# Row sums taken out of the values products, a normalisation in turned 32x32 blocks, score products dealt out over the PSUM banks, ScalarE's root and an earlier part of the ranks, in a six-stage decoder on one core

## What is computed

```python
x = _layernorm(x + _L0_attn_ref(x, ...))    # stage a: 16 heads of 128, window 64
x = _layernorm(x + _L0_xattn_ref(x, ctx))   # stage b: 16 heads of 16, causal
x = _layernorm(x + _L0_ffn_ref(x, ...))     # stage c: 8 experts, top 2
x = _layernorm(x + _L1_attn_ref(x, ...))    # stage d: 32 heads of 8, 8 kv heads, causal
x = _layernorm(x + _L1_xattn_ref(x, ctx))   # stage e: latent attention, 1601 keys
x = _layernorm(x + _L1_ffn_ref(x, ...))     # stage f: 16 heads of 16 with rms norms, then stage g: 8 experts
```

```python
scores = einsum('bhqd,bhkd->bhqk', qh, kh) * hd ** -0.5
attn   = softmax(where(causal, scores, min))
out    = einsum('bhqk,bhkd->bhqd', attn, vh)
```

## Time and profile before

| | before |
|---|---|
| median of 3 runs | 1814.74 us |
| lowest and highest | 1813.94, 1819.88 us |
| the profiled execution's own time | 1813.53 us |
| span of its trace | 1812.3 us |
| mean granted TensorE clock | 0.976 |
| PE busy | 1701.6 us (94%) |
| PEld busy | 1497.3 us (83%) |
| DVE busy | 1442.3 us (80%) |
| ACT busy | 1198.2 us (66%) |
| POOL busy | 810.8 us (45%) |

### The profile page before, as it was taken

One profiled execution on the slowest core, in us unless ns is written; L12 is line 12 of the kernel. 1 busy time (PEld: TensorE's weight loads), 2 busy tenths in 40 slices (PEclk: granted clock), 3 DMA queues, 4 the chain that ended last, 5 costly groups with the idle time before them and its releaser, 6 DMA issues.

```text
span 1812.3 us, 42783 instructions
## 1 busy us (share of the span) xinstructions
PE 1701.6 (94%) x15680; PEld 1497.3 (83%) x15680; DVE 1442.3 (80%) x3572; ACT 1198.2 (66%) x2998; POOL 810.8 (45%) x720
## 2 busy tenths in 40 slices
PE   7999999989999999899999999999999997897994
PEld 6999977758867776799999999999999996774883
DVE  5777757859856866799999999999999997686995
ACT  5766754326634543588888888888888885532663
POOL 5744422248844432444444444444444431224874
PEclk8999999989999999899999999999999999998998
DMA  5000019232338000000000000000000003302233
GB/s 175 25 1 1 1 72 361 79 99 45 54 73 265 11 3 2 24 12 13 13 12 13 30 13 13 13 13 13 12 13 1 1 2 134 158 2 86 45 54 70
DMA packets 51867, 91.74 MB, mean 51 GB/s; under 512 B 4592, under 2 KB 43632, under 8 KB 49232
## 3 DMA queue, kind: packets, MB, share of 16 engines
q1 hardware_dynamic: 42928, 78.16, 12.9%
q0 software_dynamic: 8160, 10.29, 3.7%
q10 hardware_dynamic: 576, 0.56, 0.1%
HBM read 56.13 MB, written 32.87 MB: 49 GB/s over the span
## 4 chain that ended last, share of the span: by engine, by line
PE 76%; DVE 11%; issue 4%; ACT 4%; DMA 3%; POOL 2%; SPq 0%; DVEq 0%; ACTq 0%; POOLq 0%
PE bank L100 63%; PE bank L2647 10%; DVE a_t L707 1%; PE bank L1923 1%; PE bank L1175 1%; DVE a_t L704 1%; DMA g_sums<-g_y,g_xs 1%; DMA c_sums<-c_y,c_xs 1%; POOL c_rows L1789 1%; PE bank L1895 1%; PE bank L505 1%; DVE tiny L133 1%; ACT a_OT_hi L614 0%; ACT a_P L631 0%; DVE b_nm L1444 0%
## 5 line engine op out<-in xcount | busy, mean ns | idle before, releaser
L2747 ACT ACTIVATE e_P<-bank,e_st 128x496 f32<-128x496 f32 (+2 forms) x512 | 306.3, 600 | 32.5 <-DVE e_st L2829 32.5
L2825 DVE TENSOR_REDUCE e_st<-bank 128x1 f32<-128x496 f32 (+2 forms) x512 | 288.3, 571 | 35.0 <-PE bank L100 24.8
L2848 DVE TENSOR_TENSOR e_PT_lo<-bank,e_PT_hi 128x512 fp32r<-128x512 f32 (+1 forms) x448 | 281.0, 644 | 30.9 <-ACT e_PT_hi L2767 29.9
L2647 PE MATMUL bank<-ident,e_P 128*128 128x128 f32 (+1 forms) x1664 | 257.1, 274 | 4.0 <-DVE e_PT_lo L2848 3.9
L2767 ACT CAST e_PT_hi<-bank 128x512 fp32r<-128x512 f32 (+1 forms) x448 | 247.4, 554 | 18.3 <-PE bank L2647 10.8
L100 PE MATMUL bank<-e_PT_hi,e_kv 128*128 128x256 f32 (+1 forms) x832 | 232.1, 300 | 3.1 <-DVE e_cx_lo L2855 3.1
L100 PE MATMUL bank<-e_PT_lo,e_kv 128*128 128x256 f32 (+1 forms) x832 | 214.9, 279 | 0.0
L100 PE MATMUL bank<-e_KT,e_qk_hi 128*128 128x496 f32 (+2 forms) x512 | 208.5, 407 | 6.5 <-ACT e_P L2747 3.4
L2647 PEld LDWEIGHTS bank<-ident,e_P 128*128 128x128 f32 (+1 forms) x1664 | 197.7, 140 | 17.5 <-issue 3.1
L100 PE MATMUL bank<-e_KT,e_qk_lo 128*128 128x496 f32 (+2 forms) x512 | 178.5, 349 | 0.0
L100 PEld LDWEIGHTS bank<-e_PT_hi,e_kv 128*128 128x128 f32 (+1 forms) x832 | 156.9, 189 | 8.5 <-DVE e_cx_lo L2855 3.8
(11 more groups left out here) (489 smaller groups left out, 5353.7 us busy)
## 6 DMA issues: line engine op xcount, KB each, us to landing
c_wall<-in_c_w SPq DMA_DIRECT2D x8, 1536.0 KB, 19.0
g_wall<-in_g_w SPq DMA_DIRECT2D x8, 1536.0 KB, 19.3
c_rows<-normed SPq DMA_DIRECT2D x9, 1040.0 KB, 12.9
g_rows<-normed SPq DMA_DIRECT2D x9, 1040.0 KB, 13.4
e_stage<-in_e_w SPq DMA_DIRECT2D x16, 416.0 KB, 3.2
c_xs<-c_rows SPq DMA_DIRECT2D x23, 130.0 KB
g_xs<-g_rows SPq DMA_DIRECT2D x23, 130.0 KB
landing<-in_a_wo SPq DMA_DIRECT2D x2, 1024.0 KB, 6.1
```

What stands on the lines that cost most here:

```text
L2647: last = pe.transpose(o[0:rows, c * SEQ + i * P:c * SEQ + (i + 1) * P], p[:, i, k0:k0 + rows], ident[:])
L2747: act.activation(Pm[u % 2][:, i, STARTS[j]:STARTS[j] + n], bank[score_bank[j]][:, 0:n], ACT.Exp, bias=s[:, i, 4:5], accum_out=s[:, i, j:j ...
L2825: last = dve.tensor_reduce(s[:, i, j:j + 1], bank[score_bank[j]][:, 0:PIECES[j]], AX.X, ALU.max)
L2848: dve.tensor_tensor(lo, bank[tb_bank[at % 2]][0:rows, 0:n * SEQ].rearrange("p (c n) -> p c n", c=n), hi.bitcast(F32), ALU.subtract).then_i ...
```

## The change

1. `values`: the eight products with `ones` go, and so do that tile and its memsets. Two columns per V slot are set to one (two strided memsets of GpSimd), so that in a block of 32 rows the 16 rows that hold no output hold the row sums. The units of a pair or four are shared between two accumulations, `outs[0]` and `outs[1]`, the two halves of bank 6. The first unit's values wait for `inverted`, which the first instruction of `normalise` now signals.
2. `normalise`: VectorE turns the whole bank in blocks of 32 x 32 (`transpose`, PSUM to `lifted`, 128 x 512), takes two small reciprocals of the sums (8 elements of each partition in b and f, 16 in d), multiplies in two instructions of 128 elements, and turns the result back into O (128 x 256), with two waits on its own semaphore between. The halves do the same on half of the columns each.
3. `scores`: where both kinds of scores are made (58 of the 64 units), the 24 products go in six groups of four; a group has four different row tiles and four different banks, and each from the third on waits for the last product of the group two before it, so four waits in place of one.
4. `ranks(g)`: the products of ones for the tiles before n0 go ahead of the wait for `marked(g + 1)`; behind it stand two products.
5. `experts`: in c's norm of batch 0 and in `last_norms` ScalarE takes the root (`Sqrt`, with a dummy call ahead of it), VectorE the reciprocal and one `newton` step, in place of the guess and three steps.

```diff
         V = [A(f"V{i}", [P, 2, kv_heads, slot]) for i in range(2)]
-        ones = A("ones", [P, slot])
...
             PT = [A(f"PT{i}", [P, 3, 4, P])[:] for i in range(2)]
-        inv = [A(f"inv{i}", [P, SEQ]) for i in range(2)]
+        lifted = A("lifted", [P, 2 * SEQ])[:].rearrange("p (r q f) -> p r q f", r=2, f=32)
+        inv = A("inv", [P, 2, SEQ // 32, 16 // hd])
...
         A_BANK, B_BANK, OUT_BANK, SIDE = 0, 3, 6, 7
-        outs, sums = bank[OUT_BANK][:, 0:SEQ], bank[OUT_BANK][:, SEQ:2 * SEQ]
+        outs = [bank[OUT_BANK][:, r * SEQ:(r + 1) * SEQ] for r in range(2)]
...
-            def score(n, block, j, keys_first):
+            def score(n, block, j, keys_first, opens=False):
...
                 o = bank[(B_BANK if keys_first else A_BANK) + at][:, col * P:(col + 1) * P]
-                return mm(o, k if keys_first else q, q if keys_first else k, keys_first and j == 3, True)
+                return mm(o, k if keys_first else q, q if keys_first else k, opens, True)
+            def scores_of_both(n0, n1):
+                def queries(block, j):
+                    return score(n0, block, j, False)
+                def keys(block, j, opens=False):
+                    return score(n1, block, j, True, opens)
+                queries(0, 0)
+                queries(0, 1)
+                queries(0, 2)
+                keys(1, 3, True).then_inc(half_scored.sem, 1)
+                first = half_scored.step()
+                queries(1, 0)
+                queries(1, 1)
+                keys(0, 2, True)
+                keys(0, 3, True).then_inc(half_scored.sem, 1)
+                second = half_scored.step()
+                pe.wait_ge(half_scored.sem, first)
+                queries(2, 0)
+                keys(0, 1)
+                keys(1, 2)
+                queries(2, 3).then_inc(half_scored.sem, 1)
+                third = half_scored.step()
+                pe.wait_ge(half_scored.sem, second)
+                keys(0, 0)
+                keys(1, 1)
+                keys(2, 2)
+                queries(1, 3).then_inc(half_scored.sem, 1)
+                fourth = half_scored.step()
+                pe.wait_ge(half_scored.sem, third)
+                keys(1, 0)
+                keys(2, 1)
+                queries(1, 2)
+                queries(0, 3)
+                pe.wait_ge(half_scored.sem, fourth)
+                queries(2, 1)
+                queries(2, 2).then_inc(*scored0.up())
+                keys(2, 0)
+                keys(2, 3).then_inc(*scored1.up())
...
                         pe.wait_ge(*exped.at(2 * n1))
+                if n0 is not None and n1 is not None:
+                    scores_of_both(n0, n1)
+                    return
...
                     if n1 is not None:
-                        last = score(n1, block, 3, True)
+                        last = score(n1, block, 3, True, True)
...
                 p, v = PT[n % 2], V[b % 2]
-                first, final = x == 0, x == PER - 1
+                r, rest = divmod(x, PER // 2)
...
                     pe.wait_ge(*ones_made.at(1))
-                if first and n >= PER:
-                    pe.wait_ge(*o_made.at(n // PER))
-                for into in (outs, sums):
-                    for kt in range(2):
-                        for j in range(4):
-                            h = (4 * u + j) // rep
-                            w = v[:, kt, h, at:at + 32] if into is outs else ones[:, at:at + 32]
-                            o = into[32 * j:32 * j + 32, kt * P:2 * P]
-                            x = (p[:, 2, 3, :] if kt else p[:, 0:2, 3, :]) if j == 3 else (
-                                p[:, j, 2, :] if kt else p[:, j, 0:2, :])
-                            last = mm(o, w, x, first and into is outs and kt == 0, final)
+                if x == 0 and n >= PER:
+                    pe.wait_ge(*inverted.at(n // PER))
+                for kt in range(2):
+                    for j in range(4):
+                        w = v[:, kt, (4 * u + j) // rep, at:at + 32]
+                        o = outs[r][32 * j:32 * j + 32, kt * P:2 * P]
+                        seen = (p[:, 2, 3, :] if kt else p[:, 0:2, 3, :]) if j == 3 else (
+                            p[:, j, 2, :] if kt else p[:, j, 0:2, :])
+                        last = mm(o, w, seen, x == 0 and kt == 0, rest == PER // 2 - 1)
...
                     dve.wait_ge(*summed.at(b - 1))
+                rows = bank[OUT_BANK].rearrange("p (r q f) -> p r q f", r=2, f=32)
                 for n, cols in enumerate(halves(m)):
-                    dve.reciprocal(inv[m % 2][:, cols], sums[:, cols]).then_inc(*inverted.up())
+                    q = slice(cols.start // 32, cols.stop // 32)
+                    dve.transpose(lifted[:, :, q, :], rows[:, :, q, :]).then_inc(*inverted.up())
                     dve.wait_ge(*inverted.at(m + 1 + n))
-                    dve.tensor_tensor(O[b % 2][:, c, cols], outs[:, cols], inv[m % 2][:, cols],
-                                      ALU.mult).then_inc(*o_made.up())
+                    for r in range(2):
+                        last = dve.reciprocal(inv[:, r, q, :], lifted[:, r, q, 16 - 16 * r:32 - 16 * r:hd])
+                    last.then_inc(link.sem, 1)
+                    dve.wait_ge(link.sem, link.step())
+                    for r in range(2):
+                        x = slice(16 * r, 16 * r + 16)
+                        last = dve.tensor_tensor(lifted[:, 0, q, x].rearrange("p q (x d) -> p q x d", d=hd),
+                                                 lifted[:, r, q, x].rearrange("p q (x d) -> p q x d", d=hd),
+                                                 inv[:, r, q, :].unsqueeze(3).broadcast_to(
+                                                     [P, q.stop - q.start, 16 // hd, hd]), ALU.mult)
+                    last.then_inc(link.sem, 1)
+                    dve.wait_ge(link.sem, link.step())
+                    dve.transpose(O[b % 2][:, c, cols].rearrange("p (q f) -> p q f", f=32),
+                                  lifted[:, 0, q, :]).then_inc(*o_made.up())
...
                 pool.memset(NM[x][:], 0.0).then_inc(*cleared.up())
-            pool.memset(ones[:], 0.0).then_inc(*cleared.up())
-            pool.wait_ge(*cleared.at(2 + PER + 1))
-            pool.memset(ones[:, gap:gap + hd], 1.0).then_inc(*ones_made.up())
+            pool.wait_ge(*cleared.at(2 + PER))
+            for i in range(2):
+                last = pool.memset(V[i][:, :, :, gap - 16:gap + 17:32], 1.0)
+            last.then_inc(*ones_made.up())
...
             pe.wait_ge(*self.tables_made.at(1))
+        else:
+            pe.wait_ge(*self.marked.at(g))
+        for n in range(n0):
+            mm(o[:, n0 * E:n1 * E].rearrange("p (n e) -> p n e", e=E), self.ones[:],
+               self.either[:, n:n + 1, :].broadcast_to([P, n1 - n0, E]), n == 0, False)
         pe.wait_ge(*self.marked.at(g + 1))
-        last = mm(o[:, n0 * E:n1 * E], self.earlier[:], self.either[:, n0:n1, :], True, False)
-        for n in range(n1 - 1):
-            m = max(n0, n + 1)
-            last = mm(o[:, m * E:n1 * E].rearrange("p (n e) -> p n e", e=E), self.ones[:],
-                      self.either[:, n:n + 1, :].broadcast_to([P, n1 - m, E]), False, True)
-        last.then_inc(*self.ranked.up())
+        mm(o[:, n0 * E:n1 * E], self.earlier[:], self.either[:, n0:n1, :], n0 == 0, False)
+        mm(o[:, (n1 - 1) * E:n1 * E], self.ones[:], self.either[:, n0, :], False, True).then_inc(*self.ranked.up())
...
         last_scales, odd_normed, even_normed = S_("last_scales"), S_("odd_normed"), S_("even_normed")
+        spread_known, rooted = S_("q_projected"), S_("k_projected")
...
                     upper_w(i + 1, at, 1)
+            act.activation(silu[0][:, 0:1], ident[:, 0:1], ACT.Sqrt)
+            act.wait_ge(*spread_known.at(1))
             if following:
+                act.activation(tiny[0][:, 20:22], tiny[0][:, 16:18], ACT.Sqrt).then_inc(*rooted.up())
...
             else:
+                act.activation(normal[:, TILES:2 * TILES], normal[:, 0:TILES], ACT.Sqrt).then_inc(*rooted.up())
...
+            def norm_first(T):
+                mean = T[:, 12:16].rearrange("p (t s) -> p t s", s=2)
+                v, y, s = T[:, 16:18], T[:, 18:20], T[:, 20:22]
+                row_stats(0, T)
+                dve.wait_ge(link.sem, link.value)
+                dve.tensor_scalar(v, mean[:, :, 1], EPS, None, ALU.add).then_inc(*spread_known.up())
+                dve.wait_ge(*rooted.at(1))
+                then(dve.reciprocal(y, s))
+                newton(v, y, s)
+                dve.wait_ge(link.sem, link.value)
+                for i in range(2):
+                    normed_ = dve.tensor_scalar(X[:, i, :], X[:, i, :], T[:, 12 + 2 * i:13 + 2 * i], T[:, 18 + i:19 + i],
+                                                ALU.subtract, ALU.mult)
+                normed_.then_inc(x_normed, 1)
...
                 v, s = normal[:, 0:TILES], normal[:, TILES:2 * TILES]
```

(11 more changed lines are left out.)

## The result

| | before | after |
|---|---|---|
| median | 1814.74 us (5 runs, 1810.47 to 1819.88) | 1803.90 us (5 runs, 1799.83 to 1805.17) |
| ratio of the runs | | 0.9937, interval 0.9915 to 0.9959 |
| profiled execution: span, clock | 1812.3 us, 0.976 | 1802.7 us, 0.971 |

A forecast was written before the change was run, and what follows sets the result against it. TensorE was taken as the bound, with VectorE second. Terms 20.0 + 1.3 + 3.3 + 2.0 - 0.9 - 6.3 + 0.3 + 2.3 = 22.0 us off 1814.7 gave a forecast of 1793, range 1779 to 1805.

The forecast's parts named there:

- Rival C: Normalise is dearer and VectorE binds more widely: 24 calls at 0.9 us, half exposed, 10 less gain, 1803; chance 0.16.
- D (1804): Scores: the four waits expose more than the one did, 0.23 us dearer in 50 units, 11 less, 1804; chance 0.12.
- Ones products: TensorE-bound units of b, d and f: dropping the ones group gains its whole 0.67 us in each of 27.
- Score order: Scores: two exposed waits of 0.15 us replace one of 0.37, gaining 0.07 a unit (bounds 0.37 gained, 0.23 lost).
- floor: The 19 units of b, d and f whose mask products wait for VectorE's maxima: 4.64 us, forecast 4.57.
- Normalise: VectorE's normalise: 2.20 us before, priced at 2.04 in b and f and 2.14 in d, taken as 2.1.
- VectorE's limit: Where normalise and layernorm operations lie between maxima in b, d and f, VectorE becomes the bound: 6.3 us less gain.
- The pair of the earlier trace: Two neighbouring units from 620.78 to 631.85: 11.07 us before, forecast 10.6 as VectorE binds, gaining 0.5 instead of 1.5.
- Units with a turned layernorm: The 11 units where TensorE waits otherwise for VectorE or ScalarE, mostly for that layernorm's low part: 0.3 us each, 3.3 together.
- rival E: The granted clock falls in 23 thinned units, costing 30 us, 8 more than the gain: 1823, slower; chance 0.06.
- Ranks: Stages c and g: six of eight products move ahead of VectorE's mark, 0.2 us in each, 0.3 taken for both.
- Root: From v to X's scaling at c's end, 2.38 us becomes 1.25, 1.1 less; in g 1.2 less; together 2.3.

The follow-up runs named there:

- e6: The changed kernel with the turn of the maxima moved behind the iteration's single projection or output product; 1811.10 us, ratio 0.9988 to the kernel before.
- e1: The kernel before with part 3 alone, the new order of the score products; 1812.52 us, ratio 1.0001.
- e8: The changed kernel measured again, unaltered, on another chip; 1799.73 us, ratio 0.9940 to the kernel before.
- e4: The changed kernel with normalise turning the bank in place, so that its products read PSUM; 1795.02 us, ratio 0.9905 to the kernel before.
- e5: The changed kernel with 12 or 13 idle products in the last three iterations of b, d and f; 1797.37 us, ratio 0.9917 to the kernel before.
- e12: The kernel before with parts 1 and 2 alone, sums out of the values products and normalise in turned blocks; 1803.41 us, ratio 0.9968.
- e3: The kernel before with parts 4 and 5 alone, the earlier ranks products and the root on ScalarE; 1809.40 us, ratio 0.9984.
- e9: The changed kernel with both the in-place turn in PSUM and the idle products at the stages' ends; 1794.41 us, ratio 0.9907 to the kernel before.

## Why the prediction was right in sign and twice too large

The profiles differ by 9.6 us where 22.0 were forecast. By the milestones, with the prediction's terms shared out among the stages, the missing 12.4 are: 5.0 in d's units (8.5 forecast, 3.5 measured), 4.2 between d's last maxima and f (0.4 less forecast, 3.8 more measured), 4.0 behind f (1.7 less forecast, 2.3 more measured); b, f and the stretch from b to d gave 0.8 more than forecast.

The measured 1803.9 lies where the rivals C (1803) and D (1804) stood, and what they say did not happen: normalise costs what was priced, and the waits of the new order expose 0.27 in a unit where the old one lost 0.37. So it is luck that the range, drawn to reach past D, held the time.

- *Ones products: a wait that they covered.* I priced the group at 0.67 and let a unit gain all of it, "since everything up to the mask follows in TensorE's order". The price was right: in e6, with no turn behind them, the next product starts 0.78 behind the values, against 1.43 with the ones between, 0.65 less. The order was not all: the turn also waits for ScalarE's first exponentials, which end at 0.77 and release it at 0.91. That leaves 0.53, in 27 units 3.8 us less.
- *Score order: right in the unit with the ones, smaller without.* Pauses of 0.14 and 0.13 against 0.15, gain 0.08 against 0.07 (5.90 to 5.82 in e1), floor 0.13 lower against 0.07. But 0.05 of the 0.08 goes back at the turn once the ones are gone. In the times the order showed as 0 alone and as about 2 in company.
- *Normalise: right.* 0.71 and 0.45 for the transposes against 0.69 and 0.42, 0.37 for the reciprocals against 0.45, 2.12 in all against 2.14. Rival C's price did not come. The Trainium skill's figure ("VectorE: DVE Perf Modes", The three transpose paths), scaled by size as an estimate, would have made the first 1.24; the measured 0.71 decides.
- *VectorE's limit: right in d, wrong in b.* The pair of the earlier trace rows, forecast at 10.6, answers to 612.31 to 623.93 after, 11.62: longer than the 11.07 before, with half clock in its second unit (10.62 in e8, where the clock stays up). The next pair of the kind took 10.52 (654.34 to 664.86); the wait behind its second maxima, forecast at 0.9, is 0.26, with 0.37 more for ScalarE at the turn. Three such pairs at 1.0 each are 3.0 in the sum, not 2.8. In b I took 2 us off, since VectorE had almost nothing free in the window of the earlier trace rows (28.13 less 27.6 is 0.5, not the 1 that I left it); that window went from 28.13 to 25.23 and gained all of it:

```profile
327.51:352.74 25.23, 23.36 (x356) 18.45 (x352) 23.16 (x82) 8.62 (x14) 6.16 (x10) 1.00 0.03 8
```

  Busy time plus 0.04 for each instruction would be 26.4 here, more than the window holds: that sum overstates what VectorE needs.
- *Products of two SBUF operands.* Every normalise was priced as if alone: my rows of line 1464 read PSUM, the new products read SBUF only, and I carried the price over without asking what else differed. Two units of d lost 0.9 each and the halves at d's end some 0.7 each. e4 shows it.
- *Units with a turned layernorm: overrated.* Their transposes now start behind ScalarE's second exponentials (0.41, L1399, in three of the rows), which free the bank. Five of them in d changed by -0.18 to +0.03 us each; I had given them 0.3, and one the full 0.74.
- *Clock: rival E in part.* Its chance was for a swing in all 23 thinned units; nearly all of those ran at 1.00. It fell where waits for VectorE follow one another: d's end, on the path, 3.6 us between the traces of e5 and e8; and once or twice in a round, in places that differ between the two profiles of the same kernel (one such unit of d, at 617.29, cost 1 us). As the Trainium skill has it ("TensorE: Matmul & The Clock Gate", A second HAM failure mode: psum-queue depth-cycling), short idles between groups lowered the clock, but not in the regular units at the floor, which idle for 0.36 us of 4.51.
- *Behind f: not foreseen, and open in part.* From the last maxima of f on I had 1.7 us less. The root gave its part, but the 16 scatters of stage g take 1.4 longer from first to last, and the experts behind them 1.7 longer. The first came with parts 1 and 2: 24.3 in e12, against 22.8 in e3 and 23.1 in e1. It stays in e4 and e5 (24.3 and 24.5), and is gone in e9 (22.6), which has both their edits; why, no run shows. The second varies between 142.5 and 145.7 us among kernels that don't differ there. Before and after:

```profile
L1789 POOL DMA_INDIRECT g_rows<-normed,landing x16: 966/972/1437, 1636.8 to 1659.8; - x16
L1848 POOL DMA_INDIRECT g_rows<-normed,landing x16: 967/972/1440, 1625.2 to 1649.6; - x16
```

- *Ranks: nothing.* From VectorE's mark of group 3 to its row addresses (L1774, after L1833) stage c takes 1.53 us before, 1.85 in e3 and 2.05 after, stage g 1.84, 1.84 and 1.83. In c the six products did not run ahead: TensorE was in idle products of the kernel's own, and all of the group's products started at 378.16, behind the mark.
- *Root: right.* From v to X's scaling 527.30 to 528.60, 1.30 against 1.25, 1.08 less than before; in g 1.44 where it was 2.58. In the rows of c's end after:

```profile
527.30 0.17 DVE L2175 TENSOR_SCALAR tiny<-tiny 128x2 f32<-128x2 f32 x1
527.50 0.20 ACT L2094 ACTIVATE tiny<-tiny 128x2 f32<-128x2 f32 x1 [11.99 <-DVE tiny L2175]
527.74 0.17 DVE L2177 RECIPROCAL tiny<-tiny 128x2 f32<-128x2 f32 x1 [0.27 <-ACT tiny L2094]
...
528.60 0.73 DVE L2181 TENSOR_SCALAR X<-X,tiny 128x256 f32<-128x256 f32 x2
```

Open: why the clock falls at d's end with the new score order alone, what makes the pause of 2.03 in b, and what makes the scatters of c and g longer.

## What to carry to other kernels

Before you credit a group of products at its full price, look up what the next one waits for besides its engine: a wait that the group covered comes to light when it goes. When an operation's operands move from PSUM to SBUF, look up what GpSimd does at that time before you take over its duration. And where TensorE is thinned near the end of a stage, look for half clock there, and ask of each such place whether the work behind it is on the path: in the kernel before it was free at the ends of b and f, in the changed one it was not at the end of d. Check a forecast stretch by stretch, too: two thirds of what was missing here lay not in the units that the change thins but behind d and behind f.

## What the runs showed of the hardware

- A VectorE `tensor_tensor` with both operands in SBUF, started 0.5 us into a GpSimd `tensor_tensor`, took 1.80 us for 0.49 and ended about when that did; with one operand in PSUM, at the same distance, 0.49.
- A 32 x 32 block transpose in float32: 0.71 us for 128 x 512 out of PSUM into SBUF and 0.72 back into the same bank; 0.45 for 128 x 256 in SBUF.
- Twelve or thirteen idle products in a stage's last iterations kept the clock at 1.00 there; the time of the kernel before did not move (0.9999), that of the changed one went from 0.9940 to 0.9917, with intervals that overlap.
- TensorE's waits for its own score products: a pause of 0.37 us where the wait was for the group just before (607.44 to 607.92 in the earlier trace rows, less the pitch of 0.11), 0.14 where one group of four lay between.
